# Converting half of the weight blocks behind attention on GpSimd, and the queries' normalisation moved there

## The reference

```python
x = x + tanh(g_xattn) * attention(layernorm(x), ctx, ctx)
x = x + tanh(g_ffn) * moe(layernorm(x))
```

## Time and profile before

| | us |
|---|---|
| median of 3 runs | 1272.61 (1270.43 to 1278.21) |
| span of the profiled execution | 1271.7 |
| PE busy | 1197.0 (94%) |
| DVE busy | 852.9 (67%) |
| ACT busy | 585.5 (46%) |
| POOL busy | 382.3 (30%) |

### The profile page before, as it was taken

The page is one execution under the profiler, slowest core; times in us unless marked ns, Lnnn a source line. Parts: engine busy times, 40 slices in busy tenths (PEclk is TensorE's granted clock), DMA queues, the critical chain, the costliest instruction groups (busy, mean ns, idle before and its releaser), DMA issues.

```text
span 1271.7 us, 40424 instructions
## 1 busy us (share of the span) xinstructions
PE 1197.0 (94%) x15162; PEld 889.3 (70%) x15162; DVE 852.9 (67%) x1470; ACT 585.5 (46%) x1131; POOL 382.3 (30%) x454
## 2 busy tenths in 40 slices
PE   3878889999878999999999999999999999999998
PEld 2544444555467777778888888888888888877775
DVE  5889989999887789445554455444444444447899
ACT  2767779898797422233333333333333333322221
POOL 4466766676830000210111111111111111006752
PEclk9888999999989999999999999999999999999999
DMA  5675555656665132644322454215412233057875
GB/s 183 211 247 176 176 172 187 212 186 212 209 252 190 52 133 67 225 152 152 119 82 82 139 183 157 66 58 193 146 66 66 66 125 123 33 175 234 265 227 176
DMA packets 91043, 196.32 MB, mean 154 GB/s; under 512 B 12128, under 2 KB 12640, under 8 KB 90976
## 3 DMA queue, kind: packets, MB, share of 16 engines
q1 hardware_dynamic: 80256, 160.30, 36.8%
q0 software_dynamic: 10720, 35.14, 9.2%
HBM read 331.68 MB, written 64.49 MB: 312 GB/s over the span
## 4 chain that ended last, share of the span: by engine, by line
PE 73%; DVE 12%; issue 5%; POOL 3%; DMA 3%; ACT 2%; SPq 1%; DVEq 1%; ACTq 0%; POOLq 0%
PE PS L1671 40%; PE PS L1709 20%; DVE negm L1011 5%; PE PS L1632 3%; PE PS L1484 3%; DMA qB<-negT 2%; PE PS L1518 2%; PE PS L1504 1%; ACT x2n L881 1%; POOL whl L696 1%; PE PS L1532 1%; DMA wr<-in_wr 1%; PE PS L1526 1%; DVE X L1314 1%; DVE rec L1024 1%
## 5 line engine op out<-in xcount | busy, mean ns | idle before, releaser
L1671 PE MATMUL PS<-xT,wb 128*128 128x128 f16 (+1 forms) x4128 | 279.8, 229 | 2.3 <-DVE gate L1152 1.6
L1671 PE MATMUL PS<-uhl,wb 128*128 128x128 f16 (+1 forms) x4128 | 279.8, 229 | 1.2 <-DVE uhl L1265 1.2
L1671 PEld LDWEIGHTS PS<-xT,wb 128*128 128x128 f16 x4128 | 264.1, 98 | 11.2 <-DVE gate L1152 1.7
L1671 PEld LDWEIGHTS PS<-uhl,wb 128*128 128x128 f16 x4128 | 263.5, 98 | 10.1 <-DVE uhl L1265 1.4
L1709 PE MATMUL PS<-wb,ghl 128*128 128x512 f16 x1200 | 267.2, 379 | 0.0
L1709 PEld LDWEIGHTS PS<-wb,ghl 128*128 128x128 f16 x1200 | 115.9, 98 | 130.2
L926 ACT ACTIVATE sl<-PS,bb 128x128 f32<-128x128 f32 (+1 forms) x344 | 106.7, 387 | 187.5 <-PE PS L1671 187.5
L747 POOL COPY ixr<-idx 128x2 int32 (+1 forms) x35 | 6.4, 183 | 593.3 <-PE PS L1632 593.3
L916 ACT ACTIVATE u<-PS,bb 128x128 f32<-128x128 f32 (+1 forms) x344 | 106.6, 387 | 169.5 <-PE PS L1671 164.1
L1272 DVE TENSOR_TENSOR g<-sl,u 128x512 f32<-128x512 f32 x102 | 70.5, 691 | 150.2 <-ACT sl L926 150.1
L1011 DVE TENSOR_REDUCE negm<-PS 128x8 f16<-128x1024 f32 x128 | 155.2, 1213 | 23.8 <-PE PS L1484 23.0
(11 more groups left out here) (161 smaller groups left out, 1375.9 us busy)
## 6 DMA issues: line engine op xcount, KB each, us to landing
wb<-wsc SPq DMA_DIRECT2D x219, 1024.0 KB
wst<-in_wall SPq DMA_DIRECT2D x32, 768.0 KB, 6.0
wsc<-whl SPq DMA_DIRECT2D x32, 768.0 KB, 4.3
ysl<-yb SPq DMA_DIRECT2D x43, 512.0 KB
bd<-in_bdown SPq DMA_DIRECT2D x74, 256.0 KB
X<-in_x SPq DMA_DIRECT2D x8, 1024.0 KB, 6.7
qB<-qT SPq DMA_DIRECT2D x32, 256.0 KB, 2.7
xnd<-xhl SPq DMA_DIRECT2D x32, 256.0 KB, 2.0
```

Source lines behind the costliest of these rows:

```text
L1671: ins = pe.matmul(bank_of(bank, t, m, kind), wb[:, j, l, k, w, m * P:(m + 1) * P], rhs(x, k)[:, ts], start=(n == 0), stop=(n == len(TERMS) ...
```

## The change

Six things change.

1. Blocks 0 to 14 are converted during attention, one per pair of batches instead of one per batch. Times 64 is now GpSimd's too, in the odd body; ACT's copy is at the odd body's end, GpSimd's subtraction at the start of the next even body.
2. Blocks 15 to 31 are converted behind attention by GpSimd alone, in two buffers `wst2`, `whl2` that lie where `wb`'s buffer 1 will be. SP loads the first two when all scores are done, and stores one behind each of the groups 2 to 7 of the second normalisation, then 2, 2, 2, 2 and 3 in the tiles 0 to 4, each time loading the block two on.
3. `norm1` moves from DVE to GpSimd, between `split_k` and the subtraction of `split_q`.
4. All 32 batches are written out on every engine.
5. X comes in 16 DMAs of 512 KB instead of 8 of 1 MB, one per body up to body 10; the context in 3 (4, 10 and 18 batches; the last in body 5) instead of 2 (4 and 28).
6. Buffer 0 serves tiles 0 to 6, buffer 1 tile 7 alone, loaded once all blocks are stored; the first routed expert's layers 0 and 1 are loaded behind tile 6's instead of tile 5's.

```diff
@@ -54,11 +54,13 @@
 SOON = (0, NB // 2 - 2, NB - 4, NB)
 MID = NB * P // 2
 XC = 8
+XP = NB // 2
+DURING = NB // 2 - 1
+KEPT_C = (0, 4, 14, NB)
 
 
 CHUNK = NB // XC
 KEEP = 8
...
@@ -172,6 +174,11 @@
         with ExitStack() as behind:
             yh = sb("yh", [P, 4, 2, HID], F32, behind)
         YG = [yg, yh]
+
+        with ExitStack() as spare:
+            sb("first_half", [P, 3 * KT * 2 * HID], F16, spare)
+            wst2 = sb("wst2", [P, 2, 3, HID], F32, spare)
+            whl2 = sb("whl2", [P, 2, 3, 2, HID], F16, spare)
         wb = sb("wb", [P, 2, 3, KT, 2, HID], F16)
         bb = sb("bb", [P, 2, 2, 2, KT], F32)
...
@@ -233,12 +240,7 @@
         def over_batches(eng, body):
 
 
-            for b in range(FRONT):
-                body(b // 2, b % 2, b % 4)
-            with eng.Fori(0, (NB - FRONT - 4) // 4) as i:
-                for k in range(4):
-                    body(2 * i + FRONT // 2 + k // 2, k % 2, k)
-            for b in range(NB - 4, NB):
+            for b in range(NB):
                 body(b // 2, b % 2, b % 4)
 
         def follow(half, par, quad, n):
...
@@ -262,11 +264,15 @@
             return 2 * half + par
 
 
-        def buffer(kind, half, t):
+        def buffer(kind, i, t):
 
             if kind == "early":
-                return 1 if isinstance(half, int) and half == SH_A // 2 - 1 else 0
+                return 1 if isinstance(i, int) and i == SH_A - 1 else 0
             return t if kind == "routed" else 1
+
+        def weight_block(half, quad):
+
+            return quad // 2, 8 * (half - quad // 2)
 
         def bias_slot(kind, t):
...
@@ -368,21 +376,33 @@
                 sp.wait_ge(S["negT_ready"], 2 * number(half, par) + pair + 1)
                 sp.dma_start(qB[D::STRIP, par, pair, :, :], negT[:, pair, :]).then_inc(neg_in[pair], 16)
 
-            def store_w(half, par, last):
-
-                b = number(half, par)
-                sp.wait_ge(S["wlo_ready"], b + 1)
-                sp.dma_start(wsc[bass.ds(block_of(b), 1)].rearrange("o l p r -> (o p) l r"),
-                             whl[:, par, :, :, :].rearrange("p l h c -> p l (h c)")).then_inc(w_out[par], 16)
-                if not last:
-                    load_w(b + 2, par)
+            def stored_block(n, pieces, j):
+                sp.wait_ge(S["wlo_ready"], n + 1)
+                sp.dma_start(wsc[bass.ds(block_of(n), 1)].rearrange("o l p r -> (o p) l r"),
+                             pieces[:, j, :, :, :].rearrange("p l h c -> p l (h c)")).then_inc(w_out[j], 16)
+
+            def store_w(half, quad):
+
+                j = 1 - weight_block(half, quad)[0]
+                stored_block(half - 1, whl, j)
+                if not (isinstance(half, int) and half + 1 >= DURING):
+                    load_w(half + 1, j)
+
+            def load_late(n):
+                sp.dma_start(wst2[:, n % 2, :, :], a["wall"][block_of(n)]).then_inc(w_in[n % 2], 16)
+
+            def store_late(n):
+
+                stored_block(n, whl2, n % 2)
+                if n + 2 < NB:
...
@@ -458,12 +479,14 @@
                 for r in range(4):
                     sp.wait_ge(S["x2l_ready"], 4 * i + r + 1)
                     sp.dma_start(xnd[bass.ds((4 * group_of(i) + r) * P, P), :], xhl[:, r, :, :].rearrange("p h c -> p (h c)")).then_inc(x2_out[r], 16)
-            for i in range(3):
+            sp.wait_ge(S["t_done"], UNITS * NB)
+            for n in range(DURING, DURING + 2):
+                load_late(n)
+            late = iter(range(DURING, NB))
+            for i in range(NB // 4):
                 store_x2(i)
-            store_w(NB // 2 - 1, 1, True)
-            with sp.Fori(3, NB // 4 - 1) as i:
-                store_x2(i)
-            store_x2(NB // 4 - 1)
+                if i > 1:
+                    store_late(next(late))
             for par in range(2):
                 load_bias(E_R, par, 0, always)
...
@@ -476,12 +499,14 @@
             for i in range(SH_A - 2):
                 if i > 1:
                     load_x(i + 2, i % 2, 2 * i + 4)
+                for n in range(0, 0 if i == 5 else 3 if i == 4 else 2):
+                    store_late(next(late))
+                if i == 5:
+                    for j in range(2):
+                        sp.wait_ge(w_out[j], 16 * (NB // 2))
+                    for l in range(3):
+                        first_layer(l, 1)
                 store_y(i, i % 2)
-                if i == 0:
-                    for par in range(2):
-                        sp.wait_ge(w_out[par], 16 * (NB // 2))
-                if i < 3:
-                    first_layer(i, 1)
 
             def experts(j):
...
@@ -510,16 +535,16 @@
 
             sp.wait_ge(S["phaseC"], 1)
             e = experts(0)
-            i = SH_A - 3
+            i = SH_A - 2
             sp.wait_ge(S["l1_done"], 2 * i + 2)
             load_layer(0, e[0], 0, always)
             sp.wait_ge(S["l2_done"], 2 * i + 2)
             load_layer(1, e[0], 0, always)
-            sp.wait_ge(S["l3_done"], 2 * i + 2)
-            load_layer(2, e[0], 0, always)
             i = SH_A - 1
             sp.wait_ge(S["l1_done"], 2 * i + 2)
             load_layer(0, e[1], 1, always)
+            sp.wait_ge(S["l3_done"], 2 * i)
+            load_layer(2, e[0], 0, always)
             store_y(i - 1, 0)
             for t in range(2):
                 load_bias(e[t], 0, t, always)
...
@@ -676,8 +701,16 @@
                     g.nop(nofuse=True)
                 g.tensor_tensor(kx[:, par, 1, :, 0, :], cv, kx[:, par, 0, :, 0, :], ALU.subtract).then_inc(S["k_split"], 1)
 
+            def norm1(half, par):
+                b = 2 * half + par
+
+                g.wait_ge(S["ln1_ready"], chunks_by(b))
+                need(g, S["q_split"], b - 1)
+                g.tensor_scalar(xn32[:, par, :], X[:, b, :], ln[:, 0, b:b + 1], ln[:, 1, b:b + 1], ALU.mult, ALU.add).then_inc(S["xn_ready"], 1)
+
             def split_q(half, par):
                 b = 2 * half + par
+                norm1(half, par)
                 g.wait_ge(S["qh_ready"], b + 1)
                 g.wait_ge(S["xn_ready"], b + 1)
...
@@ -690,10 +723,28 @@
                 xv = X[:, bass.ds(b, 1), :].rearrange("p o c -> p (o c)")
                 g.tensor_tensor(xv, xv, att[:, par, :], ALU.add).then_inc(S["x1_ready"], 1)
 
-            def weights_lo(half, par):
-                b = 2 * half + par
-                g.wait_ge(S["whi_ready"], b + 1)
-                g.tensor_tensor(whl[:, par, :, 1, :], wst[:, par, :, :], whl[:, par, :, 0, :], ALU.subtract).then_inc(S["wlo_ready"], 1)
+            def weights64(half, quad):
+
+                j, count = weight_block(half, quad)
+                g.wait_ge(w_in[j], count + 16)
+                if not isinstance(half, int):
+                    g.nop(nofuse=True)
+                g.tensor_scalar(wst[:, j, :, :], wst[:, j, :, :], WS, None, ALU.mult).then_inc(S["w64_ready"], 1)
+
+            def weights_lo(n, j):
+                g.wait_ge(S["whi_ready"], n + 1)
+                g.tensor_tensor(whl[:, j, :, 1, :], wst[:, j, :, :], whl[:, j, :, 0, :], ALU.subtract).then_inc(S["wlo_ready"], 1)
+
+            def late_block(n):
+
+                j = n % 2
+                g.wait_ge(w_in[j], 16 * (n // 2 + 1))
+                g.tensor_scalar(wst2[:, j, :, :], wst2[:, j, :, :], WS, None, ALU.mult).then_inc(S["w64_ready"], 1)
+                g.wait_ge(S["w64_ready"], n + 1)
+                g.wait_ge(w_out[j], 16 * (n // 2))
+                g.tensor_copy(whl2[:, j, :, 0, :], wst2[:, j, :, :]).then_inc(S["whi_ready"], 1)
+                g.wait_ge(S["whi_ready"], n + 1)
+                g.tensor_tensor(whl2[:, j, :, 1, :], wst2[:, j, :, :], whl2[:, j, :, 0, :], ALU.subtract).then_inc(S["wlo_ready"], 1)
 
             g.wait_ge(c_in[0], 16)
             values(0, 0, 0)
...
@@ -712,8 +763,10 @@
                 pv = (half - 1, 1) if par == 0 else (half, 0)
                 after = follow(half, par, quad, 2)
                 later = follow(half, par, quad, 3)
-                if not start:
-                    weights_lo(*pv)
+                if par == 0 and not start:
+                    weights_lo(half - 1, 1 - weight_block(half, quad)[0])
+                if par == 1 and not (isinstance(half, int) and half >= DURING):
+                    weights64(half, quad)
                 if after is not None:
                     values(*after)
                 if later is not None:
...
+                        g.wait_ge(c_in[c], 16)
             over_batches(g, body)
 
             residual(NB // 2 - 1, 1)
-            weights_lo(NB // 2 - 1, 1)
+            g.wait_ge(S["pv_done"], 2 * NB)
+            late_block(DURING)
             rstd2(3)
+            for n in range(DURING + 1, NB):
+                late_block(n)
 
 
             for j in range(4):
...
@@ -820,13 +877,12 @@
                 need(act, S["otr_done"], 2 * b + hf - 1)
                 act.activation(oT[:, hf, :], AT, ACT.Copy).then_inc(S["oT_ready"], 1)
 
```

(25 more changed lines are left out.)

76 lines of the change are left out of this document (34 added, 42 removed).

## The result

| us | before | after |
|---|---|---|
| median | 1271.5 (4 runs, 1270.2 to 1278.2) | 1362.5 (4 runs, 1362.1 to 1366.1) |
| profiled execution: span | 1271.7 | 1360.1 |
| TensorE's granted clock, mean | 0.984 | 0.943 |

The changed kernel takes 1.070 times as long, 95% interval 1.066 to 1.073. The direction and the place were foreseen; the size was not: 1362.5 lies above the range of 1248 to 1346.

What follows compares the result with a forecast made beforehand. Bounds: PE-DVE ping-pong in looped attention, ACT and DVE in the second normalisation, PE from the tiles on. Span 1271.7 - 23 (attention) + 21 (second normalisation) + 48 (tiles) = 1317.7, so 1318.6 us; range 1248 to 1346.

Steps and rivals of the forecast that it cites:

- The price of the late block: Behind attention: 1.5 us for each one-input GpSimd instruction, 3.1 for the subtraction; 6.2 us a block, 105 us for 17.
- the prediction's own scaling: Behind attention: losses of 69 us grow in proportion to the block's length, 6.2 us as forecast.
- Tiles 0 to 5: Eleven late blocks, 68 us of GpSimd work, collide with DVE's casts, subtractions and gating multiplies: 48 us lost.
- two ends, 33 and 68: Tiles 0 to 5: 33 us lost if DVE's idle and harmless time swallows GpSimd's work, 68 if none does.
- Second normalisation and its ends: Six late blocks at 3.6 us lose 21 us; 2 us gained as attention's last ACT and DVE conversions go.
- Attention: Gain of 7.4 in late batches, 2.6 in batch 12, 6 and 5 in the first twelve; 23 with the end's 2.
- Batch 12: Attention: written out, ACT waits only for the fourth rstd chunk instead of all eight; 2.6 of 4.0 us gained.
- 6 + 5: First twelve batches: 6 us from 1 us a pair, 5 us from fewer stalls on the maxima's DMA.
- the two-step gain of the ping-pong: Late attention batches: of four PE-DVE steps, 2.47 becomes 1.96 and 1.94 becomes 2.30; 8.85 us a batch, 7.4 gained.
- The expected stall behind x and ctx: Attention, body 5: X, 1.2 MB of context and 1.5 MB of weights queue ahead of one row of maxima.
- Rival B: Late blocks: one-input conversions run like two-input ones, 3.1 us; block 9.3, losses 104, time 1353 us; chance 0.06.
- the ends as written: Attention gain 10 to 36 us, second normalisation loss 12 to 32, tiles loss 33 to 68; range by them 1283 to 1350.

Runs made afterwards that it cites:

- part 4: Changed kernel with the late blocks' multiplication by 64 in four forms by block number, in two kernels: 1346.6 us and 1351.9 us.
- `tile_factor`: Changed kernel with every GpSimd multiplication by 64 taking its factor and an added 0 from a small tile: 1331.3 us, ratio 1.046.
- part 7: Kernel before with all batches written out, alone or with norm1 on GpSimd, finer x and ctx loads, or both: 1274.6, 1270.4, 1273.1, 1267.9 us.

## Why the prediction was wrong, step by step

**The price of the late block.** This is the step that failed: 1.5 us taken for each of the two one-input instructions, with "Ends: 1.0 us [...] and 3.1 (the two-input one)". Both ends were too low for one of them. The copy came out as worked (1.55 against 1.46 to 1.60), the subtraction too (3.1 against 3.2 to 3.4), and `norm1` took 0.77 instead of 0.64. The multiplication took 4.2. The argument "one input costs half of two" held for the copy and for `norm1`, and failed for a multiplication with no second operation. So a block was 9.0 us instead of 6.2. No row of before showed a one-operation instruction of this kind at size, and the upper end was set by the nearest slow row as if it were a ceiling. The experiments show that the missing second operation is what costs (part 4); why it does is open. The estimate from the Trainium skill ("GPSIMD Engine Reference", section "3.1 Elementwise — side-by-side cycle accounting"), 2.3 us, fits neither form: undisturbed, the runs show 4.1 with one operation and 1.5 to 1.6 with two. By the prediction's own scaling (69 x 1.5/6.2) it would also have added 17 us to the sum, not the 25 written there.

**Tiles 0 to 5: +48 predicted, +65.5 measured.** The mechanism was right in its signs (DVE's casts at 1.08 us, PE waiting for `uhl` 42 us, nothing lost from tile 6 on), though the collisions fell less on the gating than written: its multiply kept its 0.68 us, and PE waited only 6.9 us in front of the last layer. The conversion rate agrees: 48 for 68 us of GpSimd is 0.71, and 0.72 was measured. But the 48 was taken between two ends, 33 and 68, so the closeness is in part luck; `tile_factor`, with 70 us of GpSimd work, grew by 44.5. Only the 68 were 91 (the groups of lines, 42.9 + 35.5 + 16.0 in ten to eleven blocks, give 94). The 23 us more of GpSimd work, which the multiplication alone explains (10 x 2.7), are the missing 17 us at this rate.

**Second normalisation and its ends: +21 less 2 predicted, +38 measured.** One term was again the multiplication (84.5 without it: 16 us). Another was missing: I let the stage's transfers pass at nothing, having looked at the wait of SP for GpSimd alone. The six blocks' loads and stores cost 11 us with GpSimd empty. The two don't add up cleanly: with the transfers in place, the cast and the subtraction cost only 1.4 us more (84.5 against 83.1). That either hides behind the other would explain it, and is not shown.

**Attention: -21 to batch 31 predicted, -15.5 measured.** Batch 12 gave 2.7 (13.4 to 10.6) where 2.6 were written, and that is luck: ACT's wait for the rstd chunk is gone in the written-out kernels of part 7, yet their batch 12 took 11.6 to 13.1 us, as a wait of PE for GpSimd's `kx` (1.5 to 1.6 us) took its place, and with the changed attention it took 10.6 in some executions and 11.7 to 11.9 in others. The first twelve gave 9.1 for 6 + 5; part 7 finds some 4 to 6 of it in the finer loads, and how the rest splits over the reasons given is not shown. From batch 13 to batch 31 a batch went from 9.24 to 9.05 us, not 8.85 (8.97 up to batch 28), so 3.3 us came where 7.4 were written; the two-step gain of the ping-pong was worked out beside a PE that has 5% left. The expected stall behind x and ctx came once, 4.1 us of PE waiting for one row of maxima (`qB<-negT`) up to 98.16 us, inside the 127.5.

**Sum.** The misses are 5.5 + 19 + 17.5 + 0.4 = 42.4 us of span. Rival B, a block of 9.3 us, was the case that occurred (measured 9.0), for another reason than it gave; with the measured gain of 15.5 to batch 31 in place of the 21 its sum is about 1359 us, close to the result, in part by luck, as it has no term for the transfers. B was given 0.06, and the range ended below it. The range was also narrower than its own terms: the ends as written (10 gained, 32 and 68 lost) add up to 1362.6 us, not 1350, and the block's price at its upper end is not even in that. The error in the chances was to treat an unseen price as likely near the middle of its ends.

## What to carry to other kernels

An operation that the trace has never shown has no ceiling: measure it alone, or let the range reach well past the slowest relative. In these tiles work moved to GpSimd beside a busy DVE that copies and casts cost the path some 0.6 to 0.7 us for each us of GpSimd's time, however idle GpSimd was; where such a stretch is on the path, the duration on GpSimd is the price to look at, and shortening it paid at once here. An engine freed in a stretch in which another is 95% busy gave almost nothing, 0.2 us a batch.
